# Attention inside a transformer block: the weighted sum as four native 64x64 products, scores in one block, row statistics in groups

## The reference

```python
# 1 attention, 16 heads of 64, one key/value head, one null key and value per sequence
xn = ln(x, g_norm)
q = (xn @ Wq) per head;  k, v = split(xn @ Wkv)
k = concat([null_kv[0], k]);  v = concat([null_kv[1], v])
q = l2norm(q) * q_scale;  k = l2norm(k) * k_scale
sim = q @ k.T * 8 + concat([null_bias, rel_pos_bias]);  causal mask, mask
out = softmax(sim) @ v;  a = ln(out @ Wout, g_out)
# 2 retention on a:
scores = (a @ Wq.T) @ (a @ Wk.T).T * scale * decay_weights
x = x + (scores @ (a @ Wv.T)) @ Wo.T * out_scale
# 3 mixture of 8 experts (top 2) and two shared units, 4 dense layer of 1024; added to x
```

## Time and profile before

| what | value |
|---|---|
| runs | 531.86, 532.69, 539.52 us; median 532.69 |
| profiled execution, first to last instruction | 532.0 us (no other time of it is listed) |
| PE, PEld busy | 468.7 us (88%), 418.7 us (79%) |
| DVE, ACT, POOL busy | 359.7 (68%), 274.7 (52%), 284.7 (54%) us |
| chain that ended last | PE 59%, issue 8%, POOL 8%, ACT 5%, DMA 3%, DVE 3% |

### The profile page before, as it was taken

How to read it: one execution, slowest core, us unless ns; L and a number is a source line. 1 busy time by engine, 2 the same in 40 slices (tenths; PEclk the granted TensorE clock), 3 DMA queues, 4 the chain that set the end, 5 groups by cost and what they waited for, 6 DMA issues and landing times.

```text
span 532.0 us, 11898 instructions
## 1 busy us (share of the span) xinstructions
PE 468.7 (88%) x3961; PEld 418.7 (79%) x3961; DVE 359.7 (68%) x879; ACT 274.7 (52%) x574; POOL 284.7 (54%) x343
## 2 busy tenths in 40 slices
PE   3946889999999999999999896499989489999997
PEld 1735777898999988898888785398989359898986
DVE  4784888888889888898766475757664524444522
ACT  3426666576667666566652422246565234453442
POOL 3738778897987979797830777400000633425100
PEclk9966999999999999999998998989999879999999
DMA  8370103709082641000010323265752312213011
GB/s 263 90 192 1 31 1 111 257 26 343 0 292 72 208 157 30 0 30 1 1 31 2 99 100 108 82 206 185 235 169 100 89 33 57 80 41 96 25 41 39
DMA packets 51616, 52.17 MB, mean 98 GB/s; under 512 B 6645, under 2 KB 49015, under 8 KB 51577
## 3 DMA queue, kind: packets, MB, share of 16 engines
q1 hardware_dynamic: 47956, 42.98, 25.5%
q0 software_dynamic: 3072, 8.39, 5.0%
q10 hardware_dynamic: 548, 0.28, 0.2%
HBM read 22.03 MB, written 29.62 MB: 97 GB/s over the span
## 4 chain that ended last, share of the span: by engine, by line
PE 59%; issue 8%; POOL 8%; ACT 5%; DMA 3%; DVE 3%; SPq 1%; DVEq 0%; ACTq 0%; POOLq 0%
PE bank L317 10%; PE bank L318 9%; PE bank L319 9%; POOL slot_x L579 6%; PE bank L322 5%; PE bank L323 5%; PE bank L1375 3%; PE bank L1655 3%; PE bank L1400 2%; PE bank L1339 2%; PE bank L1443 2%; ACT qT L666 2%; PE bank L1351 1%; PE bank L1388 1%; DMA slot_y<-yb 1%
## 5 line engine op out<-in xcount | busy, mean ns | idle before, releaser
L588 POOL DMA_INDIRECT yg<-slot_y,yrow x32 | 34.2, 1068 | 120.8 <-DMA slot_y<-yb 76.3
L561 POOL TENSOR_TENSOR rn<-sc,half 128x6 f32<-128x6 f32 (+1 forms) x48 | 60.6, 1277 | 7.9 <-DVE sc L1023 6.9
L1256 DVE TENSOR_TENSOR hl<-hw,hh 128x512 fp32r<-128x512 f32 x32 | 22.2, 693 | 57.1 <-ACT hw L837 57.1
L835 ACT ACTIVATE hh<-bank,late 128x512 fp32r<-128x512 f32 x32 | 22.0, 688 | 53.5 <-PE bank L1655 41.9
L317 PE MATMUL bank<-wqkv_h,xnT_h 128*128 128x384 f32 x96 | 39.1, 408 | 6.8 <-DVE sim L1004 6.8
L556 POOL TENSOR_TENSOR sim<-sim,mx 128x1040 f32<-128x1040 f32 x16 | 31.3, 1955 | 23.0 <-DVE mx L1007 23.0
L695 ACT ACTIVATE sq<-bank 128x384 f32<-128x384 f32 (+1 forms) x48 | 22.8, 475 | 40.3 <-PE bank L319 24.7
L524 POOL TENSOR_TENSOR biasm<-bias,mneg 128x1040 f32<-128x1040 f32 x16 | 35.7, 2229 | 3.7 <-DMA bias<-rel_scratch 3.7
L579 POOL DMA_INDIRECT slot_x<-xs,posi x32 | 31.4, 980 | 11.2 <-issue 9.4
L542 POOL TENSOR_TENSOR pr<-pe,rden 128x1024 f32<-128x1024 f32 x16 | 30.4, 1903 | 9.2 <-DVE rden L1044 4.5
L322 PE MATMUL bank<-wout_h,oT_h 128*128 128x256 f32 x128 | 33.6, 296 | 1.9 <-DVE oT_l L1038 1.9
(11 more groups left out here) (317 smaller groups left out, 1604.8 us busy)
## 6 DMA issues: line engine op xcount, KB each, us to landing
slot_x<-zrow SPq DMA_DIRECT2D x4, 4352.0 KB, 14.4
xq<-slot_x SPq DMA_DIRECT2D x40, 128.0 KB, 2.1
slot_y<-yb SPq DMA_DIRECT2D x20, 256.0 KB, 2.4
fstage<-in_f_W SPq DMA_DIRECT2D x4, 512.0 KB, 4.5
out<-p_all SPq DMA_DIRECT2D x8, 256.0 KB, 2.1
xs<-in_x SPq DMA_DIRECT2D x1, 1536.0 KB, 9.5
raw_out<-in_c_Wout SPq DMA_DIRECT2D x1, 1024.0 KB, 7.8
stage<-in_m_wgate SPq DMA_DIRECT2D x8, 128.0 KB, 2.1
```

Of the source, the lines that this page charges most:

```text
L561: e.tensor_tensor(rn[:, lo:hi], sc[:, lo:hi], half[:, lo:hi], ALU.pow).then_inc(sems['rn'], 1)
L588: e.indirect_dma_start(out=yg[:, g % 2, r, t, :], out_offset=None, in_=ydram.ap()[:, :], in_offset=bass.IndirectOffsetOnAxis(ap=yrow[:, g ...
```

## The change

It has five parts, all in the pipeline over tiles.

1. The weighted sum takes v and the transposed weights unsplit in fp32: four products of 64 rows by 64 columns by 512 moving columns, one for each quarter of the array. For sequence 1 the heads of a pair lie swapped in the free dimension, so the bias table (three transfers instead of two), the null biases and the score order follow (`r ^ b`). `pT_l`, `vblk_h`, `vblk_l` and the zeroing go; ACT writes one `pT`; DVE writes `v_own` and `v_other`.
2. The null value is subtracted by DVE while it writes v; the product L1417 goes.
3. Scores: the last pair goes to banks 3 and 5, all 64 records stand together, the retention's products behind them. DVE adds the bias in four parts. The transposes of `pr` to bank 5 wait for DVE's second part.
4. The Wout pass with `oT_l` moves behind the q transposes. On DVE `qn` and `x1` move ahead of `den`; on ACT `kn2` moves ahead of `oT_h`.
5. The statistics and norms of x leave the steps: groups of tiles (0), (1), (2,3), (4 to 7), (8 to 11), (12 to 15), each with DVE's `row_stats(n)` at the end of its step n-2 and POOL's `norm_rows(n)` at the end of its own.

```diff
-            vblk_h, vblk_l ... nvhl, nvf ... pT_h, pT_l ... ve1, rs1, nb1, nm1
+            nvB, v_own, v_other = [P, DH], [P, 2, DH], [P, 2, DH];  pT = [P, HP, P]
+            stx, mvx, vex, rsx, nmx, nbx   # statistics and norms by tile
         def score_place(r, c):
-            return (bank[3], r * NK) if c == LAST_PAIR else (bank[2 - r], c * NK)
+            return (bank[3 + 2 * r], 0) if c == LAST_PAIR else (bank[2 - r], c * NK)
+        X_GROUPS = ((0, 1), (1, 2), (2, 4), (4, 8), (8, 12), (12, NT))
+        SCORES = ((2 * LAST_PAIR, H - 1, 3), (2 * LAST_PAIR + 1, H, 5), (1, 2 * LAST_PAIR, 1), (0, 2 * LAST_PAIR, 2))
+        SCORE_READY = (1, 1, 2, 3)
# SP
-            for b in range(2):
-                e.dma_start(bias[b * S:(b + 1) * S, :, 0:S], rel_dram.ap()...)
+            e.dma_start(bias[0:S, :, 0:S], rel_dram.ap()...)
+            for r in range(2):
+                e.dma_start(bias[S:P, :, 0:S]...[:, :, 1 - r, :], by_pair[:, :, r, :])
# POOL
+            def norm_rows(n):
+                t0, t1 = X_GROUPS[n]
+                e.wait_ge(sems['mvx'], 2 * (n + 1))
+                e.tensor_tensor(nmx[:, t0:t1], mvx[:, t0:t1, 0], fixed[:, 1:2]..., ALU.mult)
+                e.tensor_tensor(vex[:, t0:t1], mvx[:, t0:t1, 1], fixed[:, 0:1]..., ALU.add)
+                e.tensor_tensor(rsx[:, t0:t1], vex[:, t0:t1], half[:, 0:t1 - t0], ALU.pow)
+                e.tensor_tensor(nbx[:, t0:t1], nmx[:, t0:t1], rsx[:, t0:t1], ALU.mult)
             def after_first_projection():
                 e.wait_ge(sems['rn'], NB3)
-                e.wait_ge(sems['ln1_nb'], 2)
+                norm_rows(1)
                 e.wait_ge(sems['v_null'], 2)
                 e.tensor_copy(kh[:, :, S], ...).then_inc(sems['p_tables'], 1)
             def after_first_scores():
+                norm_rows(2)
             def after_second_scores():
+                norm_rows(3)
             def mask_decay():
+                norm_rows(4)
             # end of POOL's body: the per-tile norm (L562 to L570) goes
-            pipeline(e, body, {..., 2: mask_decay})
+            pipeline(e, body, {..., 2: mask_decay, 3: lambda: norm_rows(5)})
# ACT
-                    e.wait_ge(sems['ln1_nb'], due(i + 2))
+                    e.wait_ge(sems['ln1_nb'], x_groups_for(i + 1 if isinstance(i, int) else i))
...
-                        e.activation(pT_h[...], bank[4 + c]..., ACT.Copy)
+                        e.activation(pT[...], bank[4 + c]..., ACT.Copy)
# DVE
+            def row_stats(n):
+                for t in range(t0, t1):
+                    last = e.bn_stats(stx[:, t - t0, :], xs[:, t, :])
+                ...
+                for t in range(t0, t1):
+                    last = e.bn_aggr(mvx[:, t, :], stx[:, t - t0, :])
             # end of DVE's body, behind qn, x1, den and rden:
+                if live(1):
+                    e.wait_ge(sems['av_t'], due(2 * i))
+                    e.tensor_tensor(v_own[:, 1 - par, :], bank[NB3][:, values], nvB[:, :], ALU.subtract)
+                    for b in range(2):
+                        last = e.tensor_tensor(v_other[other, 1 - par, :], bank[NB3][b * S:(b + 1) * S, values], nvB[...], ALU.subtract)
+                if isinstance(i, int) and FIRST_I < i < FIRST_I + len(X_GROUPS):
+                    row_stats(i - FIRST_I)
# PE
-                    # in Wout, ahead of the transposes
+                # behind the q transposes
+                if live(-2):
+                    e.wait_ge(sems['oT_l'], due(2 * (i - 1)))
+                    for c in range(HP):
+                        last = e.matmul(bank[6][:, 0:D], oT_l[:, c, :], wout_h[:, c, :], ...)
                 def score(r, c):
-                    head = slice(r * DH, (r + 1) * DH)
                     for b in range(2):
+                        head = slice((r ^ b) * DH, ((r ^ b) + 1) * DH)
                 if live(0):
-                    score(0, LAST_PAIR).then_inc(sems['sc7'], 1)
+                    score(0, LAST_PAIR)
+                    score(1, LAST_PAIR).then_inc(sems['sim_t'], 1)
...
-                    score(1, LAST_PAIR).then_inc(sems['sim_t'], 1)      # behind the retention
...
+                        if c == 1 and live(0):
+                            e.wait_ge(sems['sim'], due(NS4 * i + 2))      # ahead of pr's transposes to bank 5
...
-                            last = e.matmul(bank[NB3][:, QB - DH:QB], ones[0:2, :], nvhl[:, :], ...)
...
-                    for b in range(2):
-                        last = split_passes(e, bank[6 + b][:, :], (vblk_h..., vblk_l...), (pT_h..., pT_l...), True, True)
-                        last.then_inc(sems['av_t'], 1)
+                    for q in range(2):
+                        rows = slice(q * S, (q + 1) * S)
+                        for b in range(2):
+                            r = q ^ b
+                            value = (v_other if r else v_own)[rows, 1 - par, :]
+                            last = e.matmul(bank[6 + b][r * DH:(r + 1) * DH, :], value, pT[rows, :, b * S:(b + 1) * S], start=True, stop=True)
+                            if q == 1:
+                                last.then_inc(sems['av_t'], 1)
```

More of the change, by code:

```diff
@@ L233, in adaln_attention_ffn @@
                     t_hT t_mlp t_fold    unit_h unit
-                    mv1 ln1_ve ln1_rs ln1_nb xn xnT xnT_h xnT_l qkv sq ss ss_c rn qn kn2 v_h
-                    kT_t kh sc7 vblk qT_t qT sim_t biasm sim mx simc pe den rden pr
-                    pT_t pT_h pT_l av_t oT_h oT_l wo_t mv2 ln2_ve ln2_rs ln2_nb zn
+                    mvx ln1_ve ln1_rs ln1_nb xn xnT xnT_h xnT_l qkv sq ss ss_c rn qn kn2 v
+                    kT_t kh qT_t qT sim_t biasm sim mx simc pe den rden pr
+                    pT_t pT av_t oT_h oT_l wo_t mv2 ln2_ve ln2_rs ln2_nb zn
                     znT_t znT uT_t uT sc_t at rt_t rT_h rT_l vo_t x1
@@ L682, in body @@
                         e.wait_ge(sems['pT_t'], due(2 * (i - 1) + c + 1))
[L683 removed]
+                        e.activation(pT[:, 4 * c:4 * c + 4, :], bank[4 + c][:, :].rearrange('p (b t) -> p b t', b=4), ACT.Copy).then_inc(sems['pT'], 1)
                 def z_copy():
@@ L1011, in body @@
                     e.tensor_tensor(rT_l[:, :, :], bank[7][:, 0:D].rearrange('p (k t) -> p k t', k=KD), rT_h[:, :, :].bitcast(F32), ALU.subtract).then_inc(sems['rT_l'], 1)
-                if live(-1):
-                    for c in range(2):
-                        e.wait_ge(sems['pT_h'], due(2 * (i - 1) + c + 1))
-                        e.tensor_tensor(pT_l[:, 4 * c:4 * c + 4, :], bank[4 + c][:, :].rearrange('p (b t) -> p b t', b=4), pT_h[:, 4 * c:4 * c + 4, :].bitcast(F32), ALU.subtract).then_inc(sems['pT_l'], 1)
                 def sums(n):
@@ L1336, in body @@
                         upper_passes(e, bank[6][:, 0:D], (wout_h[:, c, :], wout_l[:, c, :]), oT_h[:, c, :], c == 0)
-                    e.wait_ge(sems['oT_l'], due(2 * (i - 1)))
-                    for c in range(HP):
-                        last = e.matmul(bank[6][:, 0:D], oT_l[:, c, :], wout_h[:, c, :], start=False, stop=c == HP - 1)
-                    last.then_inc(sems['wo_t'], 1)
                 if live(0):
@@ L1352, in body @@
                         last.then_inc(sems['qT_t'], 1)
+                if live(-2):
+                    e.wait_ge(sems['oT_l'], due(2 * (i - 1)))
+                    for c in range(HP):
+                        last = e.matmul(bank[6][:, 0:D], oT_l[:, c, :], wout_h[:, c, :], start=False, stop=c == HP - 1)
+                    last.then_inc(sems['wo_t'], 1)
                 if live(1):
```

199 lines of the change are left out of this document (94 added, 105 removed).

## The result

| | before | after |
|---|---|---|
| median of 20 runs each, one chip, us | 532.74 | 534.59 |
| ratio of the runs, 95% interval | | 1.0053 [1.0031, 1.0076] |
| profiled execution, span, us | 532.0 | 534.7 |
| PE, DVE, ACT, POOL busy, us | 468.7, 359.7, 274.7, 284.7 | 465.0, 338.4, 258.9, 274.8 |

What follows compares the result with a forecast made beforehand. PE's own work was taken to set the pipeline loop's pace. Steady intervals -13.2, groups +7.2, start +2.5 and +1.8, drain -0.9 gave -2.6 on 532.69: 530.1 us, with an 8 in 10 range of 520 to 541.

Steps and rivals of the forecast that it cites:

- the groups' term: Three early steps with grouped statistics: `pr` waits behind POOL's norm, 17.3 us against 14.9, +7.2 in all.
- Steady step: Each later pipeline step, set by PE, goes from 14.9 to 13.7 us, between 13.4 and 14.2.
- the wait for `oT_l`: PE ahead of Wout in each step: about 0.1 us of new wait, as both halves of the weighted sum finish together.
- the sum's 1.02: The weighted sum on PE in each step: 1.15 us instead of 1.39, with ends of 0.82 and 3.28.
- the transposes and projections: PE's stretch ahead of the weighted sum: 4.73 less 0.22 for the null product, 4.51 us.
- rival D: DVE's loop binds: steady step 14.2 instead of 13.7, groups at their upper ends, 538 us; chance 0.18.
- The start: Steps 0 and 1 come later, behind statistics and norms: +2.5 and +1.8 us.
- Interval 1 to 2: From tile 1's scores to tile 2's: counted as a steady step, -1.2 us.
- B: Rival: the groups cost little since `pr` and `xn` don't come late, 517.5 us; chance 0.14.
- C: Rival: two row groups on one bank don't run together, 554 us, or 541 with the weighted sum alone; chance 0.15.
- A sum of -13.2 and +11.5: Eleven steady intervals at -1.2 us against groups +7.2 and start +2.5 and +1.8; with the drain's -0.9, -2.6.

Runs made afterwards that it cites:

- second execution: The changed kernel measured again, unchanged, on another chip: ratio 1.0042 to the kernel before (549.71 against 547.14 us).
- single tiles: The changed kernel with part 5 undone, one tile's statistics and norm in every step as before: 521.46 us, ratio 0.979.
- the groups in mid step: The changed kernel with DVE's group statistics ahead of its sums of squares and POOL's norms between `sim` and `rn`: 522.80 us, ratio 0.981.
- the pairs: The changed kernel with tiles 0 and 1 singly, then statistics and norms of two tiles in every even step: 521.26 us, ratio 0.978.
- the scores apart: The groups in mid step, with part 3 undone (last pair's second score product behind the retention's, both in bank 3): 527.59 us, ratio 0.987.
- five-group kernel: The changed kernel, `xn` in the hardware loop waiting for five groups of norms instead of six: 537.49 us, ratio 1.009; second time 1.0027.
- the one with the Wout pass back: The groups in mid step, with the `oT_l` Wout pass again ahead of the key's and q's transposes: 526.13 us, ratio 0.990.

## Why the prediction was wrong

**The step that failed is the size of the groups' term**, +7.2 for +13.9 and, in a second execution, +12.8. Its mechanism was right, also its pieces: the statistics of four tiles took 1.8 (predicted 2.1), the norm 1.7 (predicted 1.65), `pr` behind the norm, PE idle 4.0 us ahead of `pr`'s transposes (predicted 2 to 4). Two things were missing in it.

**A second waiter.** The term followed one thing that waits for the group, `pr`, and took for granted that `xn` has its norm long before. That holds in the steps that are written out. In the loop the wait counts all six groups, so `xn` of tile 5 waits for tiles 12 to 15, and `kh` and `qT` behind it. Where `xn` is let go, the two intervals that it reaches are 2.8 and 2.9 us shorter. The line that holds it (`else len(X_GROUPS)`) stands in `x_groups_for` of the changed kernel; the shortened diff ahead only calls it.

**A granted clock that falls**, which the sum put at nothing. PE idles 4 to 5 us in these steps and the clock is then at the half level, 1.2 GHz:

```profile
74.10:80.90 6.80, 5.97 (x23) 5.88 (x23) 1.98 (x7) 2.10 (x5) 4.29 (x7) 0.50 0.00 0
```

PE stood from 70.9 to 74.93 about its start; a second stretch at 0.50, of 6.8 us from 111.7, began while it stood from 107.8 to 112.76; one of 3.4 us, from 94.6, came with waits of 1.5 and 1.0. The eight transposes of `pr` at 74.93 took 1.97, those at 186.31 1.04. The Trainium skill, TensorE: Matmul & The Clock Gate, section Why this matters for your kernels, warns of idle gaps between bursts of products for this reason; the trace agrees. The price: PE's products of the three intervals took 47.3 us and, in the second execution, 46.7, against 40.7 with single tiles and 40.8 with the groups in mid step, both at a clock of 1.00. That is 6.6 and 6.0 us, as much as the whole excess over the prediction (6.7 and 5.6). In the first execution it adds to the time in full, since PE does not wait inside these stretches: from `pr`'s transposes to the weighted sum it takes 7.17 and 5.71 us (74.93 to 82.10, 95.23 to 100.94), where the steady step takes 4.38, and from the transposes of `xn` to the first projection 5.93 (112.76 to 118.69), where it takes 3.36. The two causes overlap: of the 2.8 to 2.9 us of `xn`, 2.0 to 2.5 are shorter busy time of PE. In every trace with the groups at the end of the step at least two of the three intervals hold such stretches; of the other versions, only the pairs and the scores apart have one, in the first interval (mean clock 0.90). But no run keeps these waits and a clock of 1.00 in all three: that the waits bring the stretches is read from where they stand, and not shown by itself.

**What is left of the term.** As an estimate, the five-group kernel's three intervals at full clock would be 54.51 - 3.4 = 51.1 (its products took 44.1), near the 51.9 of three intervals of 17.3: for `pr` alone the chain was right. The term counts each of them against 14.9, though the first took 16.37 before; by its own 17.3 it should have been +5.7. The upper bound, +3.5 a step, was too low for both missing causes.

**Steady step: right.** 13.73 on average for 13.7. The components are within 0.15, but for the wait for `oT_l`, 0.4 instead of 0.1; the sum's 1.02 (predicted 1.15) and the transposes and projections, 4.38 (predicted 4.51), made up for most of it. DVE's loop does not bind, rival D falls. What it gives, -11.9, was forecast to 0.1.

**The start: +2.7 for +4.3.** The first key transpose came at 30.10 (predicted 30.4), `xn` of step 1 behind its group at 52.91, PE idle for it 4.4 us; the second tile's scores at 54.88 (predicted 56.5). The gap is that work ahead of it went faster: the next key transpose at 45.63 instead of 48.31; by what is open. The prediction's terms add up to 30.3 and 52.0 where it has 30.4 and 52.1, which changes nothing. Interval 1 to 2: 14.88, not 13.85, at a clock of 0.81.

**The rivals.** B (groups cost little, 517.5) was wrong for this change, but the place decides: in mid step intervals 2 to 5 are 45.37, only 1.4 above the 43.98 of single tiles. C (quadrants pair up) falls on two rows: 64 score records with both row groups in each bank in 1.09 (184.67 to 185.76), 60 before in 1.08; and the sum in 1.02, near its lower bound of 0.82 and under the 1.64 of two by two, each bank written from both row groups in different partition halves. The rule in the Trainium skill, TensorEngine Tiling (Array Packing), Gotcha 1: PSUM Pressure, does not hold in these rows, at least where the partitions differ; the measurement decides.

**The range held the time, the direction was wrong.** A sum of -13.2 and +11.5 that leaves -2.6 has an error of several us, and its sign was worth little.

## What to carry to other kernels

When work moves to the end of a step, list everything that waits for its semaphore, on every engine, and what stands behind each waiter: two waiters on one late event can cost more than one, if one's queue feeds what the other needs next (here 2.8 us). Price a wait of PE with what follows it: here its products ran at half level behind waits of 1 to 5 us, and that cost as much as the sum was off. A wait whose count is computed from the step can be exact in written-out steps and coarse in a hardware loop; read it at the loop's first step. Place small work in the idle time that a row shows ahead of a named wait (here POOL's 1.59 us ahead of `sim`), not where the text has room for it: the same groups gave +0.5% at the end of the step and -1.9% in mid step.

## What the runs showed of the hardware that was not expected

What follows the pipeline is the same work in all versions, yet its length differs with the granted clock. From the last scores to the end, in the changed kernel and with the groups in mid step:

```profile
267.12:534.70 267.58, 238.00 (x1656) 211.39 (x1655) 139.57 (x339) 113.93 (x216) 78.80 (x82) 0.95 0.28 90
```

```profile
249.24:522.50 273.26, 241.08 (x1656) 214.75 (x1655) 140.60 (x339) 113.94 (x216) 79.91 (x82) 0.93 0.28 88
```

The kernel with the scores apart took 275.10 us there, at a clock of 0.93, with the same number of PE records. The three differ only in the pipeline. PE's busy time rises with the length, 238.0, 241.1 and 243.7. The clock does not order all kernels: the one with the Wout pass back has 269.05 us at 0.94, the kernel before 269.38 at 0.96. So up to 7.5 us of a version's time are decided behind the stage that was changed, and a gain or loss of 1% in one stage should be read in that stage's windows. Why the clock falls more often in one than in another was not tried.
